# Moving the state's products, x1's transposes and one GELU tile inside a software pipeline over 16 sequences

## The reference

```
x = layernorm(x + attn(x));  x = layernorm(x + ffn(x))

attn: q, k, v = rms_norm(x, gamma) @ (w_q, w_kv), 8 heads of 16; q = q / 4
      phi(u) = [1, u, (u_i * u_j) / sqrt 2 for all i, j]
      state[h] = sum over tokens of phi(k) (x) v;  ksum[h] = sum over tokens of phi(k)
      out = (phi(q) @ state) / max(phi(q) . ksum, 1e-5) @ w_out
ffn:  h = silu(x @ w1 * s1) * (x @ w2 * s2)
      h = gelu(h @ h1 * hs1);  h = gelu(h @ h2 * hs2);  y = h @ w3 * s3    (128 -> 512 -> 512 -> 512 -> 128)
```

## Time and profile before

| | us |
|---|---|
| median of three runs | 674.25 (674.05 to 674.5) |
| the profiled execution, as a run | 673.98 |
| its span, first to last instruction | 672.2 |
| PE busy | 595.6 (89%) |
| ACT busy | 485.9 (72%) |
| DVE busy | 458.5 (68%) |
| POOL busy | 162.3 (24%) |

### The profile page before, as it was taken

How to read it: one execution, slowest core, us unless ns; L and a number is a source line. 1 busy time by engine, 2 the same in 40 slices (tenths; PEclk the granted TensorE clock), 3 DMA queues, 4 the chain that set the end, 5 groups by cost and what they waited for, 6 DMA issues and landing times.

```text
span 672.2 us, 12074 instructions
## 1 busy us (share of the span) xinstructions
PE 595.6 (89%) x3921; PEld 430.9 (64%) x3921; DVE 458.5 (68%) x1037; ACT 485.9 (72%) x970; POOL 162.3 (24%) x216
## 2 busy tenths in 40 slices
PE   2555999999899999989999999989999998999994
PEld 2324676676667576766757667666757766676763
DVE  3555574959678595858769585966859596776673
ACT  2746568785868869586876878687787958687663
POOL 3733121221323031222303123131313113220100
PEclk9976899999999999999999999999999999999998
DMA  7000000100101010000100000000001000000000
GB/s 249 1 0 17 2 17 1 34 1 1 32 0 31 0 31 0 24 8 0 31 0 31 0 31 0 0 31 0 31 0 31 0 4 27 1 17 1 17 16 17
DMA packets 7367, 12.36 MB, mean 18 GB/s; under 512 B 816, under 2 KB 1840, under 8 KB 7344
## 3 DMA queue, kind: packets, MB, share of 16 engines
q1 hardware_dynamic: 7344, 12.06, 5.7%
HBM read 7.86 MB, written 4.19 MB: 18 GB/s over the span
## 4 chain that ended last, share of the span: by engine, by line
PE 50%; ACT 27%; issue 12%; DVE 4%; POOL 1%; ACTq 1%; POOLq 0%; DVEq 0%
PE fps L419 13%; PE fps L420 12%; ACT phiT L628 7%; PE ring L373 5%; PE ring L381 4%; ACT hid_hi L666 4%; ACT fps L667 3%; ACT L650 3%; PE ring L309 2%; PE ring L406 2%; PE ring L389 2%; PE ring L316 2%; DVE hid_lo L878 2%; PE ring L328 2%; ACT qT L620 1%
## 5 line engine op out<-in xcount | busy, mean ns | idle before, releaser
L419 PE MATMUL fps<-hid_hi,w_hi 128*128 128x512 f32 x576 | 236.2, 410 | 25.9 <-DVE hid_lo L878 24.5
L420 PE MATMUL fps<-hid_lo,w_hi 128*128 128x512 f32 x576 | 226.6, 393 | 0.0
L419 PEld LDWEIGHTS fps<-hid_hi,w_hi 128*128 128x128 f32 x576 | 108.2, 188 | 58.5 <-DVE hid_lo L878 37.9
L878 DVE TENSOR_TENSOR hid_lo<-fps,hid_hi 128x512 fp32r<-128x512 f32 x128 | 88.2, 689 | 72.7 <-ACT fps L667 72.0
L666 ACT ACTIVATE hid_hi<-fps,col 128x512 fp32r<-128x512 f32 x128 | 90.7, 708 | 63.0 <-PE fps L420 62.7
L420 PEld LDWEIGHTS fps<-hid_lo,w_hi 128*128 128x128 f32 x576 | 108.6, 189 | 18.8
L860 DVE SCALAR_TENSOR_TENSOR h<-fps,col,gate_zo 128x512 f32<-128x512 f32 x64 | 47.9, 749 | 72.5 <-ACT gate_zo L657 72.5
L667 ACT ACTIVATE fps<-fps,col 128x512 f32<-128x512 f32 x128 | 87.2, 681 | 0.0
L248 DVE TENSOR_TENSOR phi_k<-phi_k 128x896 f32<-128x896 f32 x64 | 77.4, 1211 | 5.1 <-ACT v_one L598 5.0
L628 ACT ACTIVATE phiT<-ring 128x512 f32<-128x512 f32 x128 | 73.3, 647 | 6.2 <-PE ring L328 6.2
L657 ACT ACTIVATE gate_zo<-fps,col 128x512 f32<-128x512 f32 x64 | 43.9, 686 | 36.1 <-PE fps L420 36.1
(11 more groups left out here) (111 smaller groups left out, 997.0 us busy)
## 6 DMA issues: line engine op xcount, KB each, us to landing
x_b<-in_x SPq DMA_DIRECT2D x16, 256.0 KB, 2.9
out<-gate_zo SPq DMA_DIRECT2D x16, 256.0 KB, 3.0
h<-in_h SPq DMA_DIRECT2D x1, 1024.0 KB, 7.9
gate_zo<-in_h SPq DMA_DIRECT2D x1, 1024.0 KB, 9.9
wide<-in_w SPq DMA_DIRECT2D x3, 256.0 KB, 4.4
sel_raw<-in_sel SPq DMA_DIRECT2D x1, 384.0 KB, 3.8
w_qkv_raw<-in_w_kv SPq DMA_DIRECT2D x1, 128.0 KB, 2.5
const<-in_consts SPq DMA_DIRECT2D x1, 115.0 KB, 2.6
```

Of the source, the lines that this page charges most:

```text
L419: nc.tensor.matmul(fps[:, bank, :], w_hi[:, o:o + P], hi, start=start, stop=False)
L420: mm = nc.tensor.matmul(fps[:, bank, :], w_hi[:, o:o + P], lo, start=False, stop=stop and not with_lo)
L878: nc.vector.tensor_tensor(lo, fps[:, bank, :], hi.bitcast(F32), ALU.subtract)\
```

## The change

Line numbers in the code after are other than before; the names are the same. The edits, one by one:

1. PE: `state` for sequence t moves from the start of step t+1 to the end of step t, between `sq6` and the third part of layer 4. ACT's copy of it moves with it, between the squarings of `sq6` and `sq7`, behind the load of the SiLU table. `transpose_state` becomes the first PE work of a step, in front of layer 1.
2. PE: `transpose_x1` moves from layer 4 into layer 3 (before its last two input tiles for `three3`). On ACT `x1_hi` stands behind the GELU of `three2`, on DVE `x1_lo` before the low part of `three3`.
3. ACT: the GELU of `two2` stands in front of `copy_q`, and the one of `two3` behind it. On PE `project_q` moves in front of the last part of `two2`. On DVE the low part of `two2` stands in front of `q_lo`.
4. The two plain copies of q^T go from ACT to DVE (`q_linear`), behind the low part of `two3`; they release q^T's bank. A new semaphore, `q_lo_ready`, lets the sums of q start at the low parts.
5. PE: the first three input tiles of `three0` and `three1` stand together ahead of `sq0`; `sq8` moves up to third place among the sums of q; the two `transpose_numden` stand together; `project_kv` for tile 2 stands in front of the third part of layer 2.
6. The bank lists follow these orders.

More of the change, by code:

```diff
@@ L43 @@
 RING = [(what, stage, n % 4) for n, (what, stage) in enumerate((
-    ("state", MIDDLE), ("stateT", MIDDLE), ("restT", MIDDLE), ("xT", FRONT), ("kv0", FRONT), ("acc0", MIDDLE),
+    ("stateT", MIDDLE), ("restT", MIDDLE), ("xT", FRONT), ("kv0", FRONT), ("acc0", MIDDLE),
     ("acc1", MIDDLE), ("kv1", FRONT),
     ("nt0", MIDDLE), ("nt1", MIDDLE), ("attT", MIDDLE), ("kv2", FRONT), ("out", MIDDLE), ("qT", FRONT), ("kv3", FRONT),
-    ("sq0", FRONT), ("sq1", FRONT), ("sq2", FRONT), ("sq3", FRONT), ("sq4", FRONT), ("sq5", FRONT), ("sq6", FRONT),
-    ("sq7", FRONT), ("sq8", FRONT)))]
+    ("sq0", FRONT), ("sq1", FRONT), ("sq8", FRONT), ("sq2", FRONT), ("sq3", FRONT), ("sq4", FRONT), ("sq5", FRONT),
+    ("sq6", FRONT), ("state", FRONT), ("sq7", FRONT)))]
 FPS = [(what, stage, n % 4) for n, (what, stage) in enumerate((
@@ L51 @@
     ("yT", TAIL), ("two0", FFN), ("two1", FFN), ("two2", FFN), ("two3", FFN),
-    ("three0", FFN), ("three1", FFN), ("three2", FFN), ("three3", FFN), ("x1T", MIDDLE), ("y", FFN)))]
+    ("three0", FFN), ("three1", FFN), ("three2", FFN), ("x1T", MIDDLE), ("three3", FFN), ("y", FFN)))]
 def is_positive(count):
@@ L351, in transpose_state @@
             def transpose_state(t):
-                pe.wait_ge(ring_free[bank_of(RING, "state")], read(RING, t, "state"))
+                pe.wait_ge(ring_free[bank_of(RING, "state")], read(RING, t - 1, "state"))
                 bank_wait(RING, ring_free, t, "stateT")
@@ L539, in step @@
                     if front:
-                        sums_of_q(t, 2)
+                        sums_of_q(t, 1)
+                        sums_of_q(t, 8)
                     if ffn:
@@ L553, in step @@
                     if ffn:
-                        layer3(t, 3, (2, 3), with_lo)
+                        layer4(t, (1,), with_lo)
                     if front:
                         sums_of_q(t, 6)
[L557 to L562, removed]
+                        state(t)
                     if ffn:
@@ L675, in step @@
             def step(t, par, front, middle, ffn, tail):
-                if middle:
-                    ring_copy(t, "state", st[:, :, :].rearrange("p g f -> p (g f)"),
-                              ring[:, bank_of(RING, "state"), 0:2 * FEAT])
                 if ffn:
@@ L722, in step @@
                     gelu(t, 1, 0)
-                if front and not is_step(t, B - 1):
-                    square(t + 1, 1 - par)
                 if front:
@@ L728, in step @@
                     gelu(t, 1, 1)
+                if front and not is_step(t, B - 1):
+                    square(t + 1, 1 - par)
                 if front:
-                    square_sums(t, 2, 3)
+                    square_sums(t, 8, 2)
                 if ffn:
                     gelu(t, 1, 2)
+                if middle:
+                    x1_hi(t)
                 if front:
-                    square_sums(t, 4, 5)
+                    square_sums(t, 3, 4)
                 if ffn:
@@ L737, in step @@
                 if front:
-                    square_sums(t, 6, 7)
-                if middle:
-                    x1_hi(t)
+                    square_sums(t, 5)
                 if middle:
@@ L743, in step @@
                 if front:
-                    square_sums(t, 8)
+                    square_sums(t, 6)
+                    ring_copy(t, "state", st[:, :, :].rearrange("p g f -> p (g f)"),
+                              ring[:, bank_of(RING, "state"), 0:2 * FEAT])
+                    square_sums(t, 7)
                 if ffn:
@@ L924, in step @@
                     sum_x1(t, 1 - par)
+                if ffn:
+                    gelu_tile(t, 0, 2)
                 if front:
@@ L936, in step @@
                     norm_scale(t - 1, x1p, mv, rstd, mv_ready, rstd_ready, x1[1 - par], x1_ready)
+                if ffn:
+                    gelu_tile(t, 1, 0)
                 if front:
@@ L1015, in spread_rest @@
             def spread_rest(t):
-                pool.wait_ge(ring_free[bank_of(RING, "state")], read(RING, t, "state"))
+                pool.wait_ge(ring_free[bank_of(RING, "state")], read(RING, t - 1, "state"))
                 part, whole = st_rest[:, :].ap[0], st_rest[:, :]
```

52 lines of the change are left out of this document (25 added, 27 removed).

## The result

| | before | after |
|---|---|---|
| median, us | 674.23 (674.05 to 674.5, 4 runs) | 652.16 (651.75 to 652.78, 4 runs) |
| ratio to before, 95% interval | | 0.9673 (0.9656 to 0.969) |
| span of the profiled execution | 672.2 | 650.6 |
| PE busy | 595.6 (89%) | 586.3 (90%) |
| ACT, DVE, POOL busy | 485.9, 458.5, 162.3 | 467.5, 470.1, 147.8 |

The change makes the kernel 3.3% faster, 22 us. The predicted time was 651.3.

The account below looks back on a forecast made before the run. PE, busy 89%, was taken as the bound, held by waits that trace to ACT's late 12.83 us stretch. 14 x 1.69 = 23.7, less 0.8 at the start, gives 22.9 us off: 651.3, own range 646 to 657, whole 645 to 662.

Parts of the forecast that it names:

- (a): PE in layer 3: the 1.13 us idle at the third input tile goes whole, and no new wait replaces it.
- (b): Start of ACT's busy stretch: the GELU of `three0` starts at 366.25 instead of 367.82, 1.57 us earlier.
- (c): ACT's 12.83 us stretch keeps the same set of work; the next SiLU starts at 379.08 instead of 380.65.
- (d): End of step: state's products may wait 0.4 us for a bank; PE waits 0.85 at the transposes, until 378.18.
- (e): Sum for a full step: `apply_main` starts at 381.98 instead of 383.67, 1.69 us earlier a step.
- (f): DVE's new copies out of PSUM: 0.42 to 0.69 us each, 0.69 taken; 0 to 0.5 of PE's waiting moves to `three3`.
- (g): Start and end of the kernel: -0.9 to +2.1 us in all, +0.8 taken; the last three steps 0.
- 1 (all waits go): PE is never held in a full step: 14 x 2.9 = 40.6 us gained, so 633; chance 5%.
- rival 2: DVE becomes late in the third layer, PE waits 1.75 us for the bank of `three0`: 664 us; chance 15%.
- 4: Slower: same place as rival 2, DVE later still; at 3.0 us late the time is 681; chance 3%.
- 3 (the wait only moves): ACT's stretch starts as late as before and PE stands where it stood: within 1 us of 674; chance 3%.

Follow-up runs that it names:

- u12: Kernel after with four copies of q^T on ACT in front of the GELU of `two2` again (parts 3 and 4 undone): 673.57 us, 0.9984 of before.
- u3: Kernel after with the state's products and ACT's copy back at the start of the step (part 1 undone): 662.67 us, 0.9828 of before.
- f1: Kernel after with ACT's square of the next x moved in front of the squaring of `sq0`: 645.56 us, 0.9562 of before.
- s1: Kernel after with ACT's weight casts (step 0) and DVE's first largest-value reduction (step 1) moved earlier: 647.74 us, 0.9602 of before.
- u2: Kernel after with the two copies of q^T into `restq` on ACT again (part 4 undone): 659.29 us, 0.9767 of before.

## Why the prediction was right

By its steps:

- (a), the wait at the third input tile: gone whole, in all 14 steps. u12 brings the 1.13 back. Shown. What the prediction left out is that either half alone would do two thirds of it (0.92 or 1.00 of 1.43): it sized the GELU's move and the shorter copies as one.
- (b), start of ACT's stretch: 3.70 behind the first product of layer 3, forecast 3.75.
- (c), the stretch keeps its length: 12.94, forecast 12.83, no idle time in it (in u3, without part 1, ACT does idle in it). f1 shows that its length is the pace: 0.54 less of it made the step 0.51 shorter.
- (d), state and transposes: forecast 378.18, measured 378.17. The wait of PE is 0.67 idle, and the 0.17 of overlap makes the 0.85 forecast. The state's wait for its bank, 0.35, forecast 0.4. That the products in their new place cover ACT's GELU of `three3` was in the sum only by (d)'s counts; u3 shows it as the second large piece, 0.73 a step.
- (e), 1.69 a step: measured 23.70 / 14 = 1.69. The mechanism earns the agreement to a tenth; the agreement to a hundredth is luck. The first SiLU comes 0.06 later than forecast (379.14), since the stretch starts 0.05 earlier and is 0.11 longer, and `st` starts 0.10 earlier (377.62).
- (f), DVE's copies: 0.67 and 0.69 against 0.42 to 0.69. The float32 rule of the Trainium skill ("VectorE: DVE Perf Modes", "Why PSUM operands drop a tier") is borne out by these rows. `three3` does not wait; its margin is 0.2. The low part of `three0` ended at 369.21 by the prediction's times, against 370.0 from the upper prices, since the phi_k behind the copies took 1.27 and not 1.52, and `norm_scale` 1.11 and not 1.39.
- (g), the start: mis-sized. I took +0.8; the profiled execution shows +2.04, inside the bounds of -0.9 to +2.1, at their end. The terms that cost time came: PE is 1.31 behind at the state's rest (bounds 0.3 to 1.2), and, after `apply_main` of step 1 has given 0.73 of it back (2.78 against 3.51), 1.20 behind at the largest value. The gain that I set against them, the products of step 1 out of the way of the stall, did not come. They did run early and fast (2.29 instead of 3.28). But the stall at the branch grew from 2.13 to 3.26, and layer 1, which now stands first behind it, runs slowly in their place: its matmuls last 0.63 at a granted clock of 0.52 from 72.8 to 76.2, near the lower of the clock's two levels (1.2 of 2.4 GHz), after PE had idled the 3.26. In the kernel before they were back at 0.40 by 73.79. So layer 1 starts 1.45 later than before (71.64, now 73.09), and `apply_main` of step 2 2.04 later. Why the stall grew no experiment asked. s1, which goes beyond the old order, is worth 3.9 to 4.4.
- Sum: 22.9 forecast, 22.1 measured between the medians and 21.6 between the profiled executions: the 14 steps gave the 23.7 of the forecast, the start took 1.2 more than I had set down for it, and the end 0.06.
- Rivals: 1 (all waits go) fell, since PE still waits 1.0 idle a step. Its sentence that only shorter instructions on ACT would give part of it is wrong: f1 gives 0.51 a step by moving one of them into ACT's idle time. 2 and 4 (DVE late at `three3`) did not happen, but with 0.2 of margin they named the nearest place. 3 (the wait only moves) is close to what u12 shows: with ACT's stretch starting late, parts 1, 2 and 5 bring 0.27 a step, 0.16% in the median.

## What to carry to other kernels

When PE waits for a chain of three engines, look for the engine whose timeline has no idle time between two events, and count what starts that stretch and what stands in it; here some 12.9 us of ACT's queue paced the step, and what left it (0.54, for 0.51 a step) or started it earlier (1.62, for 1.69) counted nearly in full, once per step. Work without a deadline (a copy, the next tile's square) belongs in that engine's idle time, and independent PE work in front of the product that waits for it. Moves can be worth little alone (0.27 a step for parts 1, 2 and 5) and much together, or take the place of one another (parts 3 and 4), so the kernel without one of them and the kernel without both are each worth a run.

## What the runs showed of the hardware

- POOL and DVE: one of POOL's products of 128x128 (L1010, L1009 before) took 0.49 in the full step after. In the same place before, beside a phi_k on DVE with two inputs in SBUF, it took 1.34, and that phi_k 1.52 (the next one, with POOL idle, 1.08):

```profile
365.12 1.34 POOL L1009 TENSOR_TENSOR phi_k<-phi_k 128x128 f32<-128x128 f32 x1
```

  Now it falls beside DVE's copies out of PSUM. The 32 products of this kind took 30.2 before and 16.5 after, 13.7 of the 14.5 us by which POOL's busy time fell with the same 216 instructions. This is the other side of the rule cited for rival 2 (the Trainium skill, "GPSIMD Engine Reference", "Specifications"), and these rows agree with it: the change made the contention less, not more. No run changes only what stands beside the product.
- The time varies from run to run of one kernel: u2's four runs are 661.47, 661.05, 657.54 and 656.8, with mean granted clocks of 0.972, 0.973, 0.979 and 0.979. Each kernel has one profile, so that this scatter lies in the start is inferred from profiles of different kernels: there the 16 matmuls of `apply_main` of step 1 took from 2.78 (after) to 3.64 (u12), where in the full steps they take 1.92. What sets it was not tried. Differences of 2 to 4 us between medians of such kernels are therefore better read from the full steps.
